# First attention phase: where TensorE's queue waits for value transposes, value sums and first scores, and when VectorE makes the low half of the queries

## The reference

```
qkv = xn @ W_qkv                       # 32 query heads, 16 key/value heads, 64 wide
scores = q @ k.T / 8 + slope[h] * (key - query), causal mask
attn = softmax(scores)
s = (attn @ v) @ W_out                 # summed over the heads
```

## Time and profile before

| | us |
|---|---|
| median of 3 runs | 3580.03 (3578.17 to 3584.44) |
| the profiled execution, its own time | 3579.9 |
| its span, first to last instruction | 3578.2 |
| TensorE busy (matmul records) | 3294.2 (92%) |
| VectorE, ScalarE, GpSimd busy | 2445.4, 2182.6, 1212.6 |

### The profile page before, as it was taken

How to read it: one execution, slowest core, us unless ns; L and a number is a source line. 1 busy time by engine, 2 the same in 40 slices (tenths; PEclk the granted TensorE clock), 3 DMA queues, 4 the chain that set the end, 5 groups by cost and what they waited for, 6 DMA issues and landing times. The chain is left out here.

```text
span 3578.2 us, 67403 instructions
## 1 busy us (share of the span) xinstructions
PE 3294.2 (92%) x19106; PEld 2558.5 (72%) x19106; DVE 2445.4 (68%) x6978; ACT 2182.6 (61%) x5051; POOL 1212.6 (34%) x1841
## 2 busy tenths in 40 slices
PE   3999999999999999997999997969999964999995
PEld 2777777777777777776888884536666654888885
DVE  4888888888888888886666664546666635666665
ACT  2777777777777777774655653216655630555553
POOL 6333333333333333333333331033222102243442
PEclk9999999999999999998999998979999976999998
DMA  2222222222222222225333342111111132554545
GB/s 68 44 56 54 55 55 54 56 53 57 52 57 51 57 51 57 51 50 170 126 130 132 118 138 70 47 47 26 27 31 25 29 101 101 165 128 125 140 123 159
DMA packets 175532, 280.43 MB, mean 78 GB/s; under 512 B 32434, under 2 KB 117170, under 8 KB 175410
## 3 DMA queue, kind: packets, MB, share of 16 engines
q1 hardware_dynamic: 160818, 258.94, 25.2%
q0 software_dynamic: 14592, 19.93, 3.4%
HBM read 159.79 MB, written 41.16 MB: 56 GB/s over the span
## 5 line engine op out<-in xcount | busy, mean ns | idle before, releaser
L706 POOL TENSOR_SCALAR at_p<-at_p,at_recip 128x128 f32<-128x128 f32 (+3 forms) x1028 | 533.7, 531 | 940.2 <-DVE at_recip L845 940.2
L839 DVE CUSTOM_DVE_ANT_0 at_p<-at_s_ps,at_bias 128x128 f32<-128x128 f32 (+3 forms) x1030 | 500.1, 486 | 277.1 <-PE at_s_ps L955 265.2
L756 ACT ACTIVATE at_p<-at_p,at_nmax 128x128 f32<-128x128 f32 (+3 forms) x1030 | 576.4, 560 | 170.7 <-DVE at_nmax L839 166.6
L962 PE MATMUL at_t_ps<-ident,at_p 128*128 128x128 f32 x2560 | 452.2, 275 | 0.4 <-POOL at_p L706 0.4
L954 PE MATMUL at_s_ps<-at_k_twice,at_q 128*128 128x128 f32 (+3 forms) x1030 | 373.7, 363 | 8.7 <-DVE at_nmax L839 1.2
L1779 DVE CUSTOM_DVE_ANT_0 aa_a_ps<-aa_a_ps,aa_hidden 128x128 f32<-128x128 f32 (+3 forms) x512 | 247.1, 506 | 176.6 <-PE aa_a_ps L1943 173.5
L955 PE MATMUL at_s_ps<-at_k_twice,at_q 128*128 128x128 f32 (+3 forms) x1030 | 332.6, 323 | 0.0
L962 PEld LDWEIGHTS at_t_ps<-ident,at_p 128*128 128x128 f32 x2560 | 305.3, 141 | 20.6 <-POOL at_p L706 0.8
L972 PE MATMUL at_o_ps<-at_pT,at_v 128*64 128x512 f32 (+3 forms) x2064 | 306.3, 439 | 0.0
L1679 ACT ACTIVATE aa_pT<-aa_b_ps 128x512 f32<-128x512 f32 (+1 forms) x384 | 196.6, 529 | 179.2 <-PE aa_b_ps L1961 176.5
L407 ACT ACTIVATE nw_h<-nw_h_ps,nw_b 128x512 f32<-128x512 f32 x192 | 132.1, 688 | 211.2 <-PE nw_h_ps L504 210.7
(11 more groups left out here) (314 smaller groups left out, 8387.9 us busy)
## 6 DMA issues: line engine op xcount, KB each, us to landing
at_k_twice<-at_k_parts SPq DMA_DIRECT2D x260, 256.0 KB, 3.7
nw_w_raw<-in_w_all_dram SPq DMA_DIRECT2D x52, 1024.0 KB, 7.4
w_raw<-in_w_dram SPq DMA_DIRECT2D x57, 768.0 KB, 5.7
nw_xh<-xh_dram SPq DMA_DIRECT2D x10, 512.0 KB, 4.2
nw_xl<-xl_dram SPq DMA_DIRECT2D x10, 512.0 KB, 4.8
at_w_raw<-in_w_heads_dram SPq DMA_DIRECT2D x18, 256.0 KB, 4.4
nw_x<-in_x_dram SPq DMA_DIRECT2D x9, 512.0 KB, 6.8
x_dram<-nw_x SPq DMA_DIRECT2D x9, 512.0 KB, 3.0
```

The lines of the kernel that those rows point to most:

```text
L706: pool.tensor_scalar(p, p, recip[:, u:u + 1], 1.0, ALU.mult, ALU.mult).then_inc(scaled, 1)
L756: act.activation(p_sb[:, u, 0:N], p_sb[:, u, 0:N], ACT.Exp, bias=nmax[:, u:u + 1], scale=-1.0, accum_out=total[:, u:u + 1]).then_inc(exped, 1)
L839: dve.tensor_tensor_reduce(out=p_sb[:, u, 0:N], in0=s_ps[u % 2][:, 0:N], in1=bias[:, u % 2, S - N:S], scale=1.0, scalar=BIG, op0=ALU.add, ...
L962: ins = pe.transpose(t_ps[u % 2][:, k * P:k * P + P], p_sb[:, u, k * P:k * P + P], ident[:])
```

## The change

In quarter 0 of the VectorE list `q_rest` comes ahead of the second `mask`. In the TensorE list no wait is dropped. The waits of `turn_v` and of `weigh` become functions of their own (`values_free`, `turned_out`) and stand between the two products of the score of unit 7. The waits for the queries and keys of the next item (`operands`) stand inside `weigh`, ahead of its last key tile (k = 3), in place of the head of quarter 1. At the start and at the end of the phase the same waits stand where they stood.

```
 VectorE, body:
                     turn_out(t, 2 * qt, par)
-                    mask(n, u + 1)
                     if qt == 0:
                         q_rest(t + 1, 1 - par)
+                    mask(n, u + 1)

 TensorE:
+            def values_free(n, out):
+                pe.wait_ge(vT_out, n + 1)
+                wait_alone(pe, proj_out, out, pe_ticks)
+            def turned_out(n):
+                pe.wait_ge(even_out, n * TT + (TT + 1))
+                pe.wait_ge(odd_out, n * TT + (TT + 1))
+            def operands(n, half):
+                pe.wait_ge(proj_out, q_count(n))
+                pe.wait_ge(k_copied[half[1]], half[0])
...
                 pe.matmul(s_ps[u % 2][:, 0:N], q, k_twice[par][:, 0, 0:N], start=True, stop=False)
+                if between is not None:
+                    between()
                 pe.matmul(s_ps[u % 2][:, 0:N], q, k_twice[par][:, 1, 0:N], start=False, stop=True).then_inc(scored, 1)
...
                 for k in range(TT):
+                    if k == TT - 1 and last is not None:
+                        last()
...
-                    if u == 0:
-                        pe.wait_ge(proj_out, q_count(t + 1))
-                        pe.wait_ge(k_copied[1 - par], (half + par) * 32 + 32)
-                    for h in range(2):
-                        score(n, n_par, u + h)
-                        turn(t, 2 * qt + h)
+                    score(n, n_par, u)
+                    turn(t, 2 * qt)
                     if qt == 0:
-                        turn_v(t + 1, 1 - par, v_count(t + 1) + (-2))
-                        weigh(t + (-1), 1 - par)
+                        def between():
+                            values_free(t + 1, v_count(t + 1) + (-2))
+                            turned_out(t + (-1))
+                        score(n, n_par, u + 1, between)
+                    else:
+                        score(n, n_par, u + 1)
+                    turn(t, 2 * qt + 1)
+                    if qt == 0:
+                        turn_v(t + 1, 1 - par)
+                        weigh(t + (-1), 1 - par, lambda: operands(t + 1, ((half + par) * 32 + 32, 1 - par)))
```

More of the change, by code:

```diff
@@ L928, in project_kv, with turn_v @@
                 project(m_ps[par], P, b)
-            def turn_v(n, par, out):
-                pe.wait_ge(vT_out, n + 1)
-                wait_alone(pe, proj_out, out, pe_ticks)
+            def turn_v(n, par):
                 for i in range(TT):
@@ L947, in project_out, with score @@
                     ins.then_inc(proj, 1)
-            def score(n, par, u):
+            def values_free(n, out):
[7 more added lines that the diff above has]
+                pe.wait_ge(k_copied[half[1]], half[0])
+            def score(n, par, u, between=None):
                 N = (u // 2 + 1) * P
@@ L963, in turn, with weigh @@
                 ins.then_inc(turned, 1)
-            def weigh(n, par):
-                pe.wait_ge(even_out, n * TT + (TT + 1))
-                pe.wait_ge(odd_out, n * TT + (TT + 1))
+            def weigh(n, par, last=None):
                 for k in range(TT):
+                    if k == TT - 1 and last is not None:
+                        last()
                     for h in range(2):
@@ L1006, in _ @@
             project(m_ps[1], 0, 0)
-            turn_v(0, 0, 1)
+            values_free(0, 1)
+            turn_v(0, 0)
             pe.wait_ge(proj_out, 2)
@@ L1022, in _ @@
                 body(j * B + (B - 1), j * PAIRS + (PAIRS - 1), 1, 1)
+            turned_out(KVH * B - 1)
             weigh(KVH * B - 1, 1)
```

## The result

The changed kernel takes 3566.04 us (median of 6 runs, 3563.45 to 3568.78); the kernel before 3581.03 us (6 runs, 3574.19 to 3584.44). The ratio is 0.996, 95% interval 0.9947 to 0.9973: 15 us faster, where 15.8 and 3564.2 us were forecast. The profiled execution took 3564.1 us in place of 3579.9.

The account below looks back on a forecast made before the run. TensorE sets the pace, so only time its array stands still can be won. Profiled 3579.9 less 15.8 at the first score, other parts at 0, gives 3564.1, to the median 3564.2 us; range 3560 to 3569, chance 0.77.

Parts of the forecast that it names:

- the three gaps: TensorE loads ahead of value transposes 0.20 us, value sums 0.15, first score 0.31; only the last called a wait.
- Step 1: VectorE: q_rest ahead of unit 7's mask ends about 0.72 us earlier; queue's release plus 0.24 gives 718.94.
- the load's floor: First score: some 0.20 us of gap stays even if the queries are early enough.
- Step 2: TensorE: query and key waits inside the sums ahead of k = 3 are met in time, at least 0.07 us of room.
- Step 3: Load of the first score: 0.125 us a body x 127 bodies = 15.8 us, the whole gain.
- Step 4: TensorE: four waits between unit 7's two products cost 0, with 0.18 us of cover.
- the slower rival: Second product of unit 7 starves behind the four waits: 0.25 us a body lost, 3596 us; chance 0.07.
- Step 5: Mask of unit 7 ends 1.39 us later, delaying ScalarE's exp; cost 0, with 0.1 us of room on ScalarE.
- Rivals: Gaps are waits, 3544, chance 0.06; second product of unit 7 starves, 3596, 0.07; gain given back, 3573 to 3579, 0.10.

Follow-up runs that it names:

- The old places of the waits: Changed kernel with the waits of the value transposes and value sums back right ahead of those: 3564.97 us, ratio to before 0.9954.
- the shape experiment: Kernel with those waits at their old places, plus value transposes on all 128 rows and 128 columns: 3572.85 us, ratio to the kernel before 0.9983.
- the waits alone: Changed kernel with VectorE's old order, q_rest after the mask of unit 7, the waits staying inside the products: 3614.5 us.
- the first and third experiments: First: kernel before with only q_rest moved ahead of unit 7's mask, 3565.17 us. Third: changed kernel, transpose and sum waits at old places, 3564.97 us.
- four to eight more: Changed kernel with four or eight more already met standalone waits between the two products of unit 7: 3603.96 and 3681.49 us.

## Why the prediction was right

- *What bounds:* the three gaps and their sizes were the right places; two of them do not depend on waits. The old places of the waits show it for both, the shape experiment shows the cause for the first. For the second the cause is argued, from a gap of the same kind at the next change of shape.
- *Step 1, the order on VectorE:* right, and it is all of the gain. The prediction's own numbers held this: released at 718.94, a wait at the old place is met ahead of the load's floor, 719.35 + 0.20 = 719.55. `q_rest` starts 1.57 us behind the second product of unit 6 (711.92 against 710.35), the mask that had its place 1.47 (717.31 against 715.84): so the queries came 0.62 us sooner, not 0.72.
- *Step 2, the wait ahead of k = 3:* it cost nothing, and 713.51 - (713.31 + 0.14) is just the 0.07 us of room in the sum, but by luck: the queries came 0.10 us later than in the sum, and the release takes 0.14 us there (seen with the waits alone), not 0.24. The two errors cancel. The luck decided little, since of a late load 0.16 us don't reach the body.
- *Step 3, the size:* forecast 15.8 us; the span fell from 3578.2 to 3562.4, 15.8, the medians by 15.0. That the profiled execution hit 3564.1 is in part luck, as the runs lie 5 us apart. The bodies are the firmer witness: 16.0 us less over them, and every first score at its floor.
- *Step 4, the waits between the products:* at no cost, with room of about 0.3 us where I had taken 0.18. I priced a wait at 0.12 us each in the slower rival; one with an increment costs 0.15.
- *Step 5, the late mask:* ScalarE kept 0.26 us at `take_kv` where I had 0.1. `take_o` started at the end of the exp, 714.80, 0.09 ahead of the accumulator's record end, and the next exp 0.48 us behind it (715.28), where I had 0.6.
- *Rivals:* none came true. The waits alone lose 34 us with the old order, so half of the change is a risk that the other half pays for. That the places of the waits are worth nothing was in the sum (cost 0), but I didn't say that the change would do as well without them, which the first and third experiments show.

## What to carry to other kernels

When an idle place of TensorE is put down to "issue", look at the records of its queue: if the wait ahead of it passed a microsecond earlier, the place is not that wait, and moving it is worth nothing; here the shape of the weights was the cause. A wait that binds is cured on the engine that is waited for, by doing the awaited step first, and the wait should stand as late as its first user, since an earlier one holds back work that didn't need it. Price a move by when the load is due ahead of its product, not by the load alone.

## What the runs showed of the hardware

At a change of the weights' shape on TensorE (128*128 to 64*128, to 128*64 and back) the next load started 0.20 us behind the start of a 128-column matmul and 0.15 behind a 64-column one, in every body of the changed kernel to within a few ns; with the shape kept, the load started together with the matmul ahead (713.31 in the shape experiment). A wait with an increment took 0.15 us of TensorE's queue (0.61 us a body from four to eight more), and the queue's waits passed 1.1 and 1.3 us ahead of the loads that they stood before. A load 0.55 us late delayed its product by 0.34 and the work behind it by 0.39.
